# Gated MLP with quantised down projection and adapter: the first weight quad in eight plain products instead of seven Strassen products, adapter groups moved in front of a quad's last product, per-token scale steps moved behind the seeds

## What is computed

```python
# 4096 tokens (2 x 2048), D = 512, FF = 2048, cond of 128 per batch
scale = cond @ norm_w.T + 1.0
h = x * (scale[:, None, :] * jax.lax.rsqrt(jnp.mean(x * x, -1, keepdims=True) + EPS))
val, gate = jnp.split(h @ up_w.T, 2, axis=-1)        # up_w: 4096 x 512
h = val * jax.nn.gelu(gate, approximate=False)
y = act_quant(h) @ weight_quant(down_w).T + x        # 127 steps per token; -1, 0, 1
# adapter, its weights made from cond:
Wd_b = Wd + 0.1 * (cond @ Wdd.T + bdd);  Wu_b = Wu + 0.1 * (cond @ Wdu.T + bdu)
out = y + relu(y @ Wd_b.T + bd) @ Wu_b.T + bu
```

## Time and profile before

| what | value |
|---|---|
| median of 3 runs | 882.64 us (877.78 to 882.78) |
| the profiled execution | 882.99 us, its span from first to last instruction 881.3 us |
| PE | 853.1 us busy, 97% of the span |
| DVE | 606.3 us busy, 69% |
| ACT | 388.9 us busy, 44% |
| POOL | 69.3 us busy, 8% |
| HBM | 206 GB/s over the span |
| PE in the span's 40 slices | 6 tenths, 8 tenths, then 9 or more |

### The profile page before, as it was taken

How to read it: one execution, slowest core, us unless ns; L and a number is a source line. 1 busy time by engine, 2 the same in 40 slices (tenths; PEclk the granted TensorE clock), 3 DMA queues, 4 the chain that set the end, 5 groups by cost and what they waited for, 6 DMA issues and landing times.

```text
span 881.3 us, 11920 instructions
## 1 busy us (share of the span) xinstructions
PE 853.1 (97%) x4023; PEld 373.9 (42%) x4023; DVE 606.3 (69%) x944; ACT 388.9 (44%) x630; POOL 69.3 (8%) x79
## 2 busy tenths in 40 slices
PE   6899999999999999999999999999999999999988
PEld 5234343444444444444434444444444444444433
DVE  5777667688988775446886564659986664435976
ACT  5477787766545442315545443216433332223000
POOL 1322222120200000000200000000200000001000
PEclk9899999999999999999999999999999999999999
DMA  9759887659679775646586684443547444432411
GB/s 351 279 184 317 314 294 277 232 181 318 243 267 342 285 272 206 226 169 223 199 307 223 226 281 145 162 144 96 179 131 227 132 155 137 133 114 72 143 73 71
DMA packets 63483, 183.50 MB, mean 208 GB/s; under 512 B 6976, under 2 KB 6976, under 8 KB 63424
## 3 DMA queue, kind: packets, MB, share of 16 engines
q1 hardware_dynamic: 63136, 182.48, 59.6%
q10 hardware_dynamic: 288, 0.26, 0.1%
HBM read 152.31 MB, written 29.36 MB: 206 GB/s over the span
## 4 chain that ended last, share of the span: by engine, by line
PE 81%; DVE 9%; issue 4%; ACT 3%; DMA 2%; SPq 0%; POOL 0%; DVEq 0%; ACTq 0%; POOLq 0%
PE aux_ps L969 9%; PE b_ps L902 8%; PE b_ps L906 8%; PE b_ps L904 8%; PE a_ps L902 6%; PE a_ps L906 5%; PE a_ps L904 5%; PE aux_ps L919 5%; PE e_ps L906 3%; PE e_ps L902 3%; PE e_ps L904 3%; PE aux_ps L1031 3%; PE c_ps L902 3%; PE c_ps L906 3%; PE c_ps L904 3%
## 5 line engine op out<-in xcount | busy, mean ns | idle before, releaser
L1346 DVE SCALAR_TENSOR_TENSOR h_ring<-v_sb,unscale,gelu 128x512 f32<-128x512 f32 x64 | 48.7, 761 | 102.7 <-ACT gelu L730 59.9
L706 ACT ACTIVATE b_ps<-a_ps 128x512 f32<-128x512 f32 x64 | 37.3, 582 | 158.1 <-PE a_ps L906 158.0
L902 PE MATMUL b_ps<-t_mov,u_l 128*128 128x512 f16 x256 | 97.0, 379 | 2.6 <-DVE c_ps L1314 2.6
L906 PE MATMUL b_ps<-t_mov,u_l 128*128 128x512 f16 x256 | 97.0, 379 | 0.0
L904 PE MATMUL b_ps<-t_mov,u_l 128*128 128x512 f16 x256 | 97.0, 379 | 0.0
L1368 DVE TENSOR_TENSOR hmax<-gelu,hmax 128x512 f32<-128x512 f32 x120 | 82.4, 687 | 6.0 <-ACT gelu L736 0.2
L969 PE MATMUL aux_ps<-h_ring,wq 128*128 128x512 f16 x384 | 84.9, 379 | 0.3
L623 POOL PARTITION_ALL_REDUCE yscale<-hmax x8 | 18.0, 2300 | 606.2 <-DVE hmax L1368 606.2
L919 PE MATMUL aux_ps<-w_ring,cond_sb 128*32 128x512 f32 x480 | 63.2, 612 | 1.4 <-DMA w_ring<-in_Wdd 1.3
L740 ACT ACTIVATE gelu<-h_ring 128x512 f32<-128x512 f32 x64 | 40.3, 630 | 54.5 <-DVE h_ring L1346 54.5
L736 ACT ACTIVATE gelu<-h_ring 128x512 f32<-128x512 f32 x64 | 40.3, 630 | 53.2 <-DVE h_ring L1354 52.0
(11 more groups left out here) (177 smaller groups left out, 1592.7 us busy)
## 6 DMA issues: line engine op xcount, KB each, us to landing
w_ring<-in_Wdu SPq DMA_DIRECT2D x64, 512.0 KB, 6.3
w_ring<-in_Wdd SPq DMA_DIRECT2D x56, 512.0 KB, 7.0
u_l<-ul_dram SPq DMA_DIRECT2D x48, 512.0 KB, 4.5
u_e<-ue_dram SPq DMA_DIRECT2D x48, 384.0 KB, 3.1
h_ring<-in_up_w SPq DMA_DIRECT2D x16, 512.0 KB, 6.7
ul_dram<-u_l SPq DMA_DIRECT2D x16, 512.0 KB, 7.0
x_sb<-in_x SPq DMA_DIRECT2D x8, 1024.0 KB, 8.1
res<-in_down_w SPq DMA_DIRECT2D x16, 512.0 KB, 6.4
```

Of the source, the lines that this page charges most:

```text
L902: pe.matmul(ps[:, :], weight(n, p, 0, k), hi, start=fresh and k == 0, stop=False, skip_group_check=True)
L906: mm = pe.matmul(ps[:, :], weight(n, p, 1, k), hi, start=False, stop=k == 1, skip_group_check=True)
L1346: dve.scalar_tensor_tensor(out=h_slot(n)[:, TB:TS], in0=v_sb[:, :], scalar=unscale[:, s // 2, j:j + 1], in1=gelu2[:, :], op0=ALU.mult, op1 ...
```

## The change

Four parts, all in the order of work and not in what comes out:

1. **Quad 0 in eight plain products** (`first_product`): two weight blocks per output and no sums of either side. They use B11 and B21 (block 0) first, then B12 and B22 (block 1). No `seed_b`, `keep_p5`, `seed_c`, `val2` for n = 0, no `fill` matmuls; products 3 and 4 of quad 0 leave quad 1, which has five products. `first_val_high`/`first_val_low` split the one weight piece that quad 0's Strassen form did not hold.
2. **Quad 0's sums later.** The later superblocks need quad 0's weight sums split and stored: `sums_high`, `sums_low` in n = 1, and `put_sums` (two more DMAs) in n = 2. T4's sum and split go to n = 1. POOL starts `weight_sums(0)` after both roots, `weight_sums(2)` after adapter group 2 and in another slot, `weight_sums(4)` after `sums_low`. `load_u(4)` goes up in SP's queue; `load_x(1, 0)` waits for the first eight splits.
3. **Adapter groups in front of a quad's last product** p7 in every quad; for n = 0, groups 0 to 3 lie between the plain products and 4 to 7 behind them.
4. **Steps behind seeds:** `scales(s, 0)` stands behind `seed_c`, `multiply1` and `running_max` of j = 2, as `scales(s, 1)` did and does in j = 1.

```diff
@@ tensor
-            product(0, 1)
+            first_product(a_ps[0], True, False, B11).then_inc(s_p[1], 1)
+            first_product(b_ps[0], True, True, B11).then_inc(s_p[5], 1)
             adapter_group(0)
             spread_rs(1)
             adapter_group(1)
+            first_product(a_ps[0], False, False, B21).then_inc(s_p[2], 1)
+            first_product(b_ps[0], False, True, B21).then_inc(s_p[4], 1)
             adapter_group(2)
             adapter_group(3)
+            bounds(-1)
+            pe.wait_ge(s_xs, 2 * KD)
+            first_product(c_ps, True, False, B12).then_inc(s_p[6], 1)
+            first_product(b_ps[1], True, True, B12)
+            first_product(c_ps, False, False, B22).then_inc(s_p[3], 1)
+            first_product(b_ps[1], False, True, B22).then_inc(s_p[7], 1)
+            for g in range(4, EARLY):
+                adapter_group(g)
...
-                product(n, 2)
-                if n == 0:
-                    adapter_group(5)
-                product(n, 7)
-                if n == 0:
-                    adapter_group(6)
-                    adapter_group(7)
-                for key in side_work(n):
-                    if key[0] == "dw":
-                        adapter_group(key[1])
-                    elif key[0] == "stat":
+                    product(n, 2)
+                    for g in groups_of_quad(n):
+                        adapter_group(g)
+                    product(n, 7)
+                for key in side_work(n)[len(groups_of_quad(n)):]:
+                    if key[0] == "stat":
@@ tensor, new
+            def first_product(ps, first_half, val, m):
+                pe.wait_ge(s_ulo, part_count(0, 0 if first_half else 2))
+                if first_half and val:
+                    pe.wait_ge(s_first_lo, 1)
...
+                pe.wait_ge(s_thi, split_count(0, m))
+                for k in range(2):
+                    pe.matmul(ps[:, :], rows(0, k), split(0, k), start=first_half and k == 0,
+                              stop=False, skip_group_check=True)
+                    pe.matmul(ps[:, :], rows(1, k), split(0, k), start=False, stop=False,
+                              skip_group_check=True)
+                pe.wait_ge(s_tlo, split_count(0, m))
+                for k in range(2):
+                    mm = pe.matmul(ps[:, :], rows(0, k), split(1, k), start=False, stop=k == 1,
+                                   skip_group_check=True)
+                return mm
@@ gpsimd
-            pool.wait_ge(s_rs, 1)
+            pool.wait_ge(s_rs, 2)
             weight_sums(0)
-            pool.wait_ge(s_rs, 2)
             weight_sums(1)
@@ scalar, ahead of the loop
+            t_high(0, T1)
+            t_high(0, T2)
+            u_high(1, 0)
+            t_high(0, T3)
+            stage_group(4)
+            u_high(1, 1)
+            gate2(0)
+            u_high(1, 2)
+            u_high(1, 3)
+            stage_group(5)
+            stage_group(6)
+            absolute1(0)
+            absolute2(0)
+            stage_group(7)
@@ scalar, in the loop, now from n = 1
-                if j == 0:
+                if j == 0 or n == 1:
                     t_high(s, T4)
...
+                if n == 1:
+                    sums_high(0)
+                    sums_high(1)
@@ vector, ahead of the loop
+            moving_sum(0, T2)
+            t_low(0, T1)
+            u_low(1, 0)
+            t_low(0, T2)
+            moving_sum(0, T3)
+            u_low(1, 1)
+            multiply1(0)
+            multiply2(0)
+            t_low(0, T3)
+            u_low(1, 2)
+            u_low(1, 3)
+            seed_c(1)
@@ vector, in the loop
-                if s > 0 and j == 2:
-                    scales(s, 0)
...
-                if s > 0 and j == 1:
-                    scales(s, 1)
+                if s > 0 and j in (1, 2):
+                    scales(s, 2 - j)
                 val2(n)
+                if n == 1:
+                    sums_low(0)
+                    sums_low(1)
@@ sync
             put_l(0)
+            load_u(4)
             move(4)
             put_e(1)
             move(5)
+            move(6)
+            move(7)
...
+                    if j == 2:
+                        put_sums()
```

290 lines of the change are left out of this document (178 added, 112 removed).

## The result

The changed kernel takes 893.32 us (median of 6 runs, 888.48 to 895.47). The kernel before, run beside it, takes 879.97 us (6 runs, 877.66 to 882.78). The ratio is 1.0147 with a 95% interval of 1.0111 to 1.0182: slower by 1.5%, 13 us by the medians. I had said 881.7 us, 876 to 887, and within 1%.

The account below looks back on a forecast made before the run. PE was busy 853.1 of 881.3 us, so only its waits or half-clock time could be won. Start -1.8, tiles +2.4 and seeds -1.7 gave -1.1 on 882.99, 881.9, taken as 881.7 us; range 876 to 887.

Parts of the forecast that it names:

- PE has no gap up to here: Start, up to groups 4 and 5 at 40.2: no PE gap; the two gaps of 2.53 and 1.3 us gone.
- Group 6 waits 1.9 and group 7 waits 2.0: Start: group 6 waits for ACT's copies from 40.2 to 42.1, group 7 from 43.1 to 45.1.
- One stretch at half the clock, 1.6 us: Behind those two waits of the start, PE's clock falls to half once, costing 1.6 us; bounds 0 to 3.
- One operation of VectorE stopped under GpSimd, 0.45: Start: of four DVE operations beside POOL's sums, one is lengthened by 0.45 us; bounds 0 to 2.9.
- rival D: The lock: POOL's sums each stop DVE's four operations in the start, 2.9 in place of 0.45; 884.2 us; chance 0.05.
- Quad 2 costs 11.5 and 2.4 of waits: Quad 2 takes 11.5 us as before, plus 2.0 for ACT's late `seed_b(2)` and up to 0.4 for tiles.
- The tiles: 1.3 in quads 7 and 9, 0 in the other seven: Superblock 0's groups need tiles one product earlier: 1.3 us lost in each of two quads, less 0.2, +2.4 us.
- rival B: Tiles late everywhere: all nine group quads of superblock 0 lose 1.3 us, 11.7 in all; 891.2 us; chance 0.10.
- the start's gain: Parts 1 and 2: quad 3 starts at 69.0 instead of 70.76, -1.8 us.
- Part 4, -1.7: Moving `scales` removes PE's seed waits of 0.86 in quad 18 and 0.88 in quad 34: -1.7 us, bounds 0 and -1.74.
- Quad 50 had no wait: In the kernel before, quad 50 had no seed wait, as an adapter product covers it.
- Rival C: The seed's wait moves on to quads 19 and 35, where `seed_c` has 0.6 us in hand; 883.4 us; chance 0.10.

Follow-up runs that it names:

- the best kernel: Changed kernel with `power(1)` first, ACT's copies of groups 4 to 7 early, quads 4-15 tiles early, superblock 3's `scales` back, groups behind last product: 874.65 us.
- the early copies: Changed kernel with `power(1)` first, groups behind the last product, and ACT's copies of groups 4 to 7 earlier in its program: 879.48 us, ratio 0.9983.

## Why the prediction was wrong, step by step

**"PE has no gap up to here" (40.2), the start.** Wrong, and the first cause. I let group 1 run right after the spread, since I laid it out by what it reads. I did not ask what must have read its bank. Bounds(-2) had written it, and its reader is `power(1)`, which the change moved behind four scalings. The gap is 3.35 us at 29.76, and `power(1)` first removes it. Behind it stand ACT's copy of group 1 and, on ACT's queue, the splits; so group 7 waited to 48.5 where I had 45.1.

**"Group 6 waits 1.9 and group 7 waits 2.0".** Right in mechanism, and in size for group 7: 0.97 and 1.83, each for ACT's copy, as the early copies show. They came 3.5 us later, by the step before.

**"One stretch at half the clock, 1.6 us".** Mis-sized. After has two stretches, by the windows above some 3.4 us before 34 and some 6.8 us from 47.6 to 54.4, and the second lies on group 7, the bounds and quad 1. The kernel with the groups put back has the same program up to quad 2 and gaps of 1.80 and 1.83 where after has 0.97 and 1.83. But it has full clock throughout in its profiled execution, and starts quad 2 at 58.23 instead of 61.15: 2.9 us, of which 0.3 was there at quad 0, for both stretches together, against my 1.6. Its windows:

```profile
48.00:50.00 2.00, 1.64 (x12) 1.00 0.34 133
50.00:52.00 2.00, 2.00 (x10) 1.00 0.06 16
52.00:54.00 2.00, 2.00 (x11) 1.00 0.69 152
```

That the clock fell in the one and not in the other, whose gaps are no shorter, also says that my step "one gap, hence one stretch" can't be relied on.

**"One operation of VectorE stopped under GpSimd, 0.45".** Right for the changed kernel, where between 30 and 45 us one operation took 1.75 in place of 1.22. GpSimd's sums of group 2 came behind the 3.35 us gap, mostly into time in which VectorE was idle or had small operations. With the gap gone they run under VectorE's, and its operations take 2.1 us more. That is the place and near the size of rival D. In turn, each engine waits for the other. These are the best kernel's rows of GpSimd, to read beside VectorE's above:

```profile
33.91 1.59 POOL L674 TENSOR_TENSOR h_ring<-h_ring 128x256 f32<-128x256 f32 x1
...
36.16 1.71 POOL L678 TENSOR_TENSOR h_ring<-h_ring 128x256 f32<-128x256 f32 x1
```

GpSimd's operation at 33.91 ends 0.58 us after VectorE's of 33.17 to 34.92, and the one at 36.16 ends 0.59 after VectorE's of 35.72 to 37.28, so it did its 0.7 us of work only then; and VectorE's next, from 37.20, is 0.53 longer. The Trainium skill (SBUF — State Buffer, Who interferes with whom) has this pair, a VectorE instruction with two SBUF inputs and a GpSimd one that reads SBUF, on one lock, and the rows agree. I had set that rule aside at 0.05 because the rows of before showed one side stretched at a time; those rows had few overlaps to show.

**"Quad 2 costs 11.5 and 2.4 of waits".** Right in size: 14.06 us. In another place, though: `seed_b(2)` held PE for 0.24 us and not 2.0. The late tiles of quad 2's groups (2.92 for 1.92) are not the reason either, as quad 2 takes 14.05 or 14.06 in all twelve kernels with the new start, groups ahead or behind. VectorE and ACT set it: `seed_c(2)` runs 8.92 us into the quad in the changed kernel and in the one with the groups put back, where it ran 5.54 us in before. Ahead of it stands the work that part 2 moved there, T4 and the sums' splits. The seed before, changed, and with the groups put back:

```profile
64.77 0.69 DVE L1314 TENSOR_TENSOR c_ps<-b_ps,p_sb 128x512 f32<-128x512 f32 x1
```

```profile
70.07 0.69 DVE L1436 TENSOR_TENSOR c_ps<-b_ps,p_sb 128x512 f32<-128x512 f32 x1
```

```profile
67.15 0.69 DVE L1436 TENSOR_TENSOR c_ps<-b_ps,p_sb 128x512 f32<-128x512 f32 x1
...
67.98 0.38 PE L989 MATMUL b_ps<-t_mov,u_l 128*128 128x512 f16 x1 [1.40 <-DVE c_ps L1436]
```

ACT's last copy of the groups ends 13.98 us into the quad in the last two, and the bounds behind it wait for it. That VectorE's and ACT's longer programs are the reason is read from these traces; no run takes the work away again, and every kernel with the new start pays these 2.5 us.

**"The tiles: 1.3 in quads 7 and 9, 0 in the other seven".** The mechanism was right, the term was mis-sized: 5.7 us in six quads. (In quad 2 the 1.0 us is hidden, as above.) I took "no row shows a late tile" for "there is room for 1.3 us". The room can be read. In the kernel before, quad 4's loads and groups are

```profile
80.64 1.92 SPq L442 DMA_DIRECT2D w_ring<-in_Wdd  x4
...
89.52 1.92 PE L919 MATMUL aux_ps<-w_ring,cond_sb 128*32 128x512 f32 x16
```

The last of the four is issued at about 82.1 (three quarters of 1.92 behind 80.64), and in that stretch a tile takes up to 7.8 us to land: 89.9. The last four matmuls start at 91.0. The room is 1.1 us, less than the 1.3 by which the group moves, and how long a tile takes also differs with what else is on the queue (8.3 us for that one in the changed kernel). This was my rival B, "tiles late everywhere", at a chance of 0.10; its condition, three late quads or more, came true. The measured time is above even its 891.2, as that sum still had the start's gain. I also left superblock 2 out: quads 35 and 38 lost 1.6 us.

**"Part 4, -1.7".** The mechanism holds (quads 18 and 34 shorter by 1.03 each, -2.1), but in the changed kernel part 3 had it already, so part 4 adds 0. I counted one wait twice: once as removed by moving `scales`, while the groups moved in front of product 7 cover it. "Quad 50 had no wait" was true, and I stopped one quad short: the wait is in quad 51, +1.4. Rival C, the wait moving on, named quads 19 and 35; these have none.

**The sum.** -1.8, +2.4 and -1.7 against +4.45, +7.3 and -0.7 (quads 18 and 34 -2.1, quad 51 +1.4), and 0.9 that quads 27 and 28 (0.7) and steps of 0.1 elsewhere gave: 10.2. The chance of 0.05 for slower by over 1% was too small, because I gave rival B as the only way there and kept my own start as certain in it. The start's 4.45 and half of B's 11.7, less part 4's 1.7, come to 8.6 us, about 1%. Nor does the range follow from its bounds: clock 0 to 3, tiles 0 to 5 and port 0 to 2.9 about 881.7 give 877.2 to 888.2, not 878.5 to 886. The measured time lies outside either.

## What to carry to other kernels

When a step moves, look at what frees its output's buffer as well as at what it reads: here a 0.14 us operation, pushed behind four others on VectorE, held a PSUM bank and cost the start 3 us. When a consumer moves forward, compute for every transfer it uses the last issue plus the longest landing, and compare that with the new time of need; a trace without waits doesn't say how much room there is. And before adding the gains of two edits, ask whether both remove the same wait.
